# The loops of three edge layers written out, and part of the weighing of gathered rows moved from VectorE to ScalarE

## The reference

```python
h = relu(layernorm(x)); x = x + L0(h)   # edge MLP, 20 kinds of products per edge, segment sum
h = relu(layernorm(x)); x = x + L1(h)   # GAT, 4 heads of 64
h = relu(layernorm(x)); x = x + L2(h)   # sum of edge_weight * (h @ w_nbr)[src], + h @ w_own + bias
h = relu(layernorm(x)); x = x + L3(h)   # graph transformer block, 8 heads of 32, two batch norms, MLP

# L1 (L3 alike, with another score and 8 heads)
e = leaky_relu(es[src] + ed[dst]); m = segment_max(e, dst)
ex = exp(e - m[dst]); alpha = ex / segment_sum(ex, dst)[dst]
out = segment_sum(alpha[:, :, None] * z[src], dst)
```

## Time and profile before

| | |
|---|---|
| median of 3 runs | 8612.5 us (8587.99 to 8642.88) |
| profiled execution, its time | 8678.63 us |
| its span | 8676.9 us |
| PE, PE weight loads, DVE busy | 68%, 50%, 60% of the span |
| ACT, POOL busy | 23%, 44% |
| mean granted TensorE clock | 0.788 |

### The profile page before, as it was taken

One profiled execution on the slowest core, in us unless ns is written; L12 is line 12 of the kernel. 1 busy time (PEld: TensorE's weight loads), 2 busy tenths in 40 slices (PEclk: granted clock), 3 DMA queues, 4 the chain that ended last, 5 costly groups with the idle time before them and its releaser, 6 DMA issues. The chain is left out here.

```text
span 8676.9 us, 128745 instructions
## 1 busy us (share of the span) xinstructions
PE 5902.0 (68%) x29234; PEld 4310.6 (50%) x29235; DVE 5168.6 (60%) x12724; ACT 1984.6 (23%) x6402; POOL 3831.7 (44%) x4450
## 2 busy tenths in 40 slices
PE   2289999999999645555556555555845555555864
PEld 1178888888888533333334333333323333333553
DVE  4757777777776445665664444444326666777445
ACT  1045555555554311111112000000111111111232
POOL 1013333333333066666660666666026656675000
PEclk7589999999999867777778666666967767777587
DMA  2121111111111333333321233333033323232200
GB/s 76 43 81 53 51 51 53 51 51 53 51 52 50 114 96 89 85 87 83 86 73 58 86 90 90 90 90 89 28 92 85 82 74 82 79 89 67 62 6 31
DMA packets 319334, 606.56 MB, mean 70 GB/s; under 512 B 92201, under 2 KB 195565, under 8 KB 318719
## 3 DMA queue, kind: packets, MB, share of 16 engines
q0 software_dynamic: 171200, 474.81, 19.8%
q1 hardware_dynamic: 140746, 123.45, 4.7%
q10 hardware_dynamic: 7200, 6.56, 0.2%
HBM read 548.80 MB, written 62.98 MB: 71 GB/s over the span
## 5 line engine op out<-in xcount | busy, mean ns | idle before, releaser
L288 POOL DMA_INDIRECT G<-table,ib x1760 | 1917.2, 1089 | 470.5 <-issue 470.5
L186 POOL DMA_INDIRECT G<-table,ib x1760 | 1684.1, 957 | 470.2 <-issue 470.2
L560 PE MATMUL pM<-G,one 128*128 128x260 f32 (+1 forms) x3520 | 1282.1, 485 | 603.5 <-issue 212.1
L215 DVE TENSOR_TENSOR acc<-acc,pM 128x512 f32 (+1 forms) x1760 | 967.1, 549 | 600.2 <-DMA xr<-x 292.0
L560 PEld LDWEIGHTS pM<-G,one 128*128 128x128 f32 x3520 | 651.8, 221 | 1092.6 <-DVE acc L425 547.8
L425 DVE TENSOR_TENSOR acc<-acc,pM 128x260 f32 (+1 forms) x1760 | 758.0, 431 | 670.6 <-PE pM L560 391.7
L638 PE MATMUL pM<-G,one 128*128 128x256 f32 x1760 | 702.3, 550 | 592.3 <-DVE one L628 405.7
L1278 ACT ACTIVATE oh<-one,a4S 128x128 f32<-128x128 f32 x2640 | 861.6, 389 | 1.1 <-issue 0.9
L638 PEld LDWEIGHTS pM<-G,one 128*128 128x128 f32 x1760 | 427.2, 267 | 867.4 <-DVE one L628 462.1
L1357 PE MATMUL pM<-prod,oh 128*128 128x64 f32 x3520 | 681.9, 275 | 0.0
L479 ACT ACTIVATE oneT<-pT 128x512 bf16<-128x512 f32 x440 | 261.8, 597 | 1771.3 <-PE pT L544 893.9
(11 more groups left out here) (309 smaller groups left out, 8619.1 us busy)
## 6 DMA issues: line engine op xcount, KB each, us to landing
G<-table,ib POOLq DMA_INDIRECT x3520
far<-step_rec SPq DMA_DIRECT2D x224, 64.0 KB
table<-row SPq DMA_DIRECT2D x100, 128.0 KB
table<-row SPq DMA_DIRECT2D x50, 132.0 KB
table<-row SPq DMA_DIRECT2D x50, 130.0 KB
base<-aux SPq DMA_DIRECT2D x50, 128.0 KB
bs<-base SPq DMA_DIRECT2D x50, 128.0 KB
x<-xo ACTq DMA_DIRECT2D x50, 128.0 KB
```

The source lines that it names most:

```text
L186: pool.indirect_dma_start(G[j][:, :], None, rows, bass.IndirectOffsetOnAxis(ap=ib[:, j:j + 1], axis=0)).then_inc(s_g[j], 16)
L215: nc.vector.tensor_tensor(at, at, pM[j % R][:, :], ALU.add).then_inc(s_acc, 1)
L288: pool.indirect_dma_start(G[:, par * C + j, 0:ROW], None, tab, bass.IndirectOffsetOnAxis(ap=ib[:, par * C + j:par * C + j + 1], axis=0)).t ...
L560: nc.tensor.matmul(pM[j % R][:, :], one[:, par * C + j, :], G[:, par * C + j, :], start=True, stop=True).then_inc(s_m, 1)
```

## The change

Three edits. `steps` passes K // u turns as written out in layer 2 (u = 16), so that its loop is gone; layer 0 (u = U = 8) keeps its loop. `over_chunks` calls every chunk in turn, with no loop, in layers 1 and 3. And the last QA quads of a full chunk (3 in layer 1, 2 in layer 3) are weighed by ACT: for each step and head one activation of 64 (layer 1) or 32 (layer 3) columns whose scale is the head's column of `G`. DVE weighs the first QV = 8 - QA. The last chunk has four quads, which DVE weighs.

```diff
-            with eng.Fori(peel, count // unroll) as i:
-                turn(i, False)
+            if peel < count // unroll:
+                with eng.Fori(peel, count // unroll) as i:
+                    turn(i, False)
...
-            pipelined(eng, K, u, 1, *parts)
+            pipelined(eng, K, u, 1 if u == U else K // u, *parts)
...
+            QA = 3 if H == 4 else 2
+            QV = C4 - QA
...
-                    for a_ in range(3):
-                        do(a_, a_ % 2, C, C if a_ else 0)
-                    with eng.Fori(1, (NC - 2) // 2) as i:
-                        for r_ in (1, 2):
-                            do(2 * i + r_, r_ % 2, C, C)
-                    for a_ in range(NC - 1, NC + 1):
-                        do(a_, a_ % 2, TAIL if a_ < NC else 0, C if a_ < NC else TAIL)
+                    for a_ in range(NC + 1):
+                        do(a_, a_ % 2, C if a_ < NC - 1 else TAIL if a_ < NC else 0, 0 if a_ == 0 else TAIL if a_ == NC else C)
...
                                 for q in range(nq):
-                                    weigh(b_, 1 - par, q)
+                                    if q < QV:
+                                        weigh(b_, 1 - par, q)
...
+                        def weigh(b_, par, q):
+                            act.wait_ge(s_al, b_ + 1)
+                            F = D // H
+                            for j in range(par * C + 4 * q, par * C + 4 * q + 4):
+                                for h in range(H):
+                                    ins = nc.scalar.activation(G[:, j, h * F:(h + 1) * F], G[:, j, h * F:(h + 1) * F], ACT.Copy,
+                                                               scale=G[:, j, D + h:D + h + 1])
+                            ins.then_inc(s_wa, 1)
...
-                            for q in range(3, mq):
-                                turned(a_, par, q)
+                            for q in range(3, C4):
+                                if q < mq:
+                                    turned(a_, par, q)
+                                if q - 3 < QA and 4 * (QV + q - 3) < n_b:
+                                    weigh(b_, 1 - par, QV + q - 3)
...
-                            if j % 4 == 0:
-                                pe.wait_ge(s_msg, C4 * b_ + j // 4 + 1)
+                            if j % 4 == 0 and j // 4 < QV:
+                                pe.wait_ge(s_msg, QV * b_ + j // 4 + 1)
+                            elif j % 4 == 0:
+                                pe.wait_ge(s_wa, QA * b_ + j // 4 - QV + 1)
```

More of the change, by code:

```diff
@@ L253, in edge_attention @@
                     se.sem(n) for n in ("s_R", "s_f", "s_bt", "s_al", "s_msg", "s_m", "s_acc", "s_rs", "s_v", "s_z", "s_rows", "s_i", "s_part"))
-                s_ed = se.sem("s_ed")
+                s_ed, s_wa = se.sem("s_ed"), se.sem("s_wa")
                 s_g = [se.sem(f"s_g{z}") for z in range(2 * C4)]
```

## The result

The changed kernel takes 8999.26 us (median of 4, 8986.29 to 9023.51), the kernel before, run beside it, 8623.76 us: ratio 1.0444, 95% interval 1.0401 to 1.0487. It is slower by 4.4%, where the prediction said 8130 us. Its profiled execution took 9023.51 us.

A forecast was written before the change was run, and what follows sets the result against it. It took POOL to bound layers 1 and 2 after the change, ACT's queue to brake layer 3. 165 + 193 + 150 = 508 us off 8678.6 (profiled) or 8612.5 (median) gives 8171 or 8105; it took 8130, range 8000 to 8330.

The forecast's parts named there:

- the supply of instructions after a jump: Layers 1 to 3: DVE's slow instructions, 0.70 us each, begin behind the loop's branch and last some 17 us.
- The jump goes, and with it the slow stretch: Layer 2 written out: no slow stretch, POOL bounds at 1126 us for 1291, -165 us.
- its like in layer 1 and 3: Layers 1 and 3 without jumps, ScalarE's weighs included: -193 us in layer 1, -150 us in layer 3.
- The sign of ScalarE's part: Layer 1: moved weighs pay by leaving POOL alone; three would have cost it 2.3 us more a chunk.
- POOL's interference: Layer 1: DVE's weighs and marks delay POOL, 0.75 us a weigh, 0.25 a mark; POOL bounds at 46.5 us a chunk.
- ACT as its brake: Layer 3: queued activations make PE wait; PE and DVE lose 5.5 us a chunk, win 1.4, giving 51.2 us.
- (4): Layers 1 and 3: written-out code from memory brings a slow stretch with each new page, 9050 us; chance 0.06.
- (2): Slow stretches don't hang on the jump and would stay in layer 2, 165 us more, 8295 us; chance 0.08.
- (1): Layer 3: ACT is no brake, activations cost 0.15 us or less, POOL bounds, 8026 us; chance 0.14.
- (3): Layers 1 to 3: straight code loses too, though less, 220 us more, 8350 us; chance 0.17.

The follow-up runs named there:

- only2: Changed kernel with layers 1 and 3 back in loops and all weighs on DVE, only layer 2 written out: 1.0004 of before, without stretches.
- only_act: Kernel before, all loops kept, with only ScalarE's weighs added in layers 1 and 3: 1.0145 of before, on a chip without stretches.
- all_dve_2: Changed kernel without ScalarE's part: loops written out, DVE weighs all eight quads; on a chip with stretches, 0.9804 of before.
- split: Written-out loops; idle ScalarE activations, later last weighs left out. Layer 3, with stretches: 51.1 us a chunk with all weighs, 61.6 with two missing.
- after_3: The changed kernel unaltered, run again on a chip without stretches: 8124.63 us, 1.0034 of before.
- all_dve: Changed kernel without ScalarE's part: loops written out, DVE weighs all eight quads; on a chip without stretches, 0.9994 of before.
- thin: Written-out loops, all weighs on DVE, layer 2 gathers 64 of 256 columns: 0.9997, then 0.9975, without stretches. As a sum in probe: 651 us.
- probe: Changed kernel with layer 2's sum replaced by eight 448-step sums, each with one thing changed; with stretches, the sums took 645 to 661 us.
- plain: The sum of probe that runs as in the changed kernel, 448 steps, on a chip with stretches: 650 us.

## Why the prediction was wrong

**The step that failed** is "I take the slow stretches for the supply of instructions after a jump", and with it "The jump goes, and with it the slow stretch" (layer 2, -165) and its like in layer 1 and 3. The reading under it, that the slow instructions "begin right behind the branch", was wrong too. In layer 2 of before, 224 of the 254 sequencer instructions over 0.5 us (the node loads left out) come 8 us or more behind DVE's last branch. One turn, the branch and the next sequencer instruction, then adds:

```profile
L133 DVEq COMPARE_BRANCH  x1: 56/56/56, 5156.1 to 5156.1; - x1
L133 DVEq FUSED_REGOPS  x1: 74/74/74, 5156.4 to 5156.4; - x1
```

```profile
5164.47 0.42 DVE L215 TENSOR_TENSOR acc<-acc,pM 128x256 f32 x1
...
5171.11 0.42 DVE L215 TENSOR_TENSOR acc<-acc,pM 128x256 f32 x1 [3.54 <-issue]
```

Between 5158 and 5164.47 the adds are 0.63 to 0.86 us apart, and the first slow one stands 8.5 us behind the branch, 9 into POOL's run of gathers. A loop's turn there is as long as a cycle of POOL's: run of gathers, stretch, pause of POOL (in 45 of 53 it begins 19 to 20 us behind DVE's branch), catch-up. The two were locked, and I took the one for the cause of the other. In layers 1 and 3 the order is the other way round. The long chunk of the earlier trace rows (3709.87 to 3772.15) lost most of its time ahead of its jump, the largest piece 17 us before it, where an add comes 8.7 us behind the one before:

```profile
3750.68 0.42 DVE L425 TENSOR_TENSOR acc<-acc,pM 128x260 f32 x1 [7.15 <-remote]
```

In layer 3 chunk 2 took 72.1 us before DVE had jumped at all. What a jump itself costs is the time from the branch to the next sequencer instruction, 3.1 us in layer 1 and 0.3 in layer 2, and it is the same on chip 9, without stretches (only2, only_act):

```profile
L264 DVEq COMPARE_BRANCH  x1: 68/68/68, 3767.8 to 3767.8; - x1
L264 DVEq FUSED_REGOPS  x1: 126/126/126, 3770.9 to 3770.9; - x1
```

The written-out layer 2 has no jump and a cycle of 28.8 us of its own. Gain in layer 2: 24 us (1291 to 1267) for 165; with loops written out and nothing else, in the profiled executions, layer 1 gained 27 x 2.2 = 59 us for 193, layer 3 27 x 6.0 = 162 (all_dve_2 against before). (The two traces may be of two chips, both with stretches.) What the runs put in its place: on some chips the engines beside POOL get late some 10 us into a run of gathers and are fast again about three us after POOL stops, in loops and in straight code alike, so that layer 2 takes some 1.44 us a step for the 1.27 I forecast.

The trace of before had shown it without any jump. Ahead of layer 1's first chunk POOL issues 64 gathers in a row (3055 to 3137 us), DVE has nothing to do from 3075 on, the code is written out, and ACT's `turned` comes ever later behind PE's product. Three rows of ACT:

```profile
3099.09 0.60 ACT L479 ACTIVATE oneT<-pT 128x512 bf16<-128x512 f32 x1 [11.99 <-DMA a_pad<-zf]
3120.09 0.60 ACT L479 ACTIVATE oneT<-pT 128x512 bf16<-128x512 f32 x1 [20.40 <-issue]
3141.79 0.60 ACT L479 ACTIVATE oneT<-pT 128x512 bf16<-128x512 f32 x1 [21.10 <-DMA a_pad<-zf]
```

In only2, on chip 9, the same rows stand 2.4 us apart. So the lateness is not DVE's alone. From the first gather to the first scores before takes 90 us there and only2 44, and in layer 3 it is 96 and 44. All eight traces with stretches have it (67 to 92 us ahead of layer 1), and none of the twelve others (44 us). These some 100 us of before were in none of my terms, and no edit of the change touches them.

**The sign of ScalarE's part.** I wrote that the moved weighs "pay here by leaving it alone", POOL that is. On a chip with stretches taking the weighs away is what costs: 8 to 9 us a chunk in layer 1, 7 to 12 in layer 3 (table), and split shows it in layer 3 with ACT idle. Without stretches the step holds: 2.5 us a chunk less in layer 1.

**The sum, where there are no stretches.** after_3 took 8124.63 us for 8130. Layer 2: 1123 us for 1126. Layer 1: 1199 us for 1415 - 193 = 1222; DVE waits for gathers as forecast, and POOL's interference was put 1.9 us a chunk too high (44.6 for 46.5). Layer 3: 1408 us for 1377, 52.5 us a full chunk for 51.2, with ACT as its brake: in the chunk from 6312.6 us PE waits 4.8 us for `oneT`, where I had 5.5. A row of ACT there:

```profile
6282.57 6.88 ACT L485 ACTIVATE G<-G 128x32 f32<-128x32 f32 x32
```

The quad took 6.88 us for my 7.0. (The Trainium skill, "ScalarE: Activation LUTs", What ACT_TABLE_LOAD costs, gave 6.8; less the last activation's 0.31 the row's 31 intervals are 0.212 us each for its 0.213, so the trace agrees.) But on those chips before takes 8078 to 8083 us: the 508 us that I meant to win were mostly stretches, and there they are gone without any edit. That 8130 was met there is luck. The misses in layers 1 and 3 (23 us too high, 31 too low) nearly cancel, and the change is worth nothing on such a chip.

**What I overlooked.** I explained the profiled execution's lying 36 us over the highest run by stretches, and so knew that they vary between executions. I did not ask whether they vary between chips.

**Rivals.** (4) gave 9050 us, and 8999 came: right in size, wrong in mechanism, since written-out code alone is 2.0% faster. I gave it 0.06 for the reason that chunks 0 to 2 ran well in straight code. That held for layer 1 alone (layer 3's chunk 2 took 72.1 us), and they ran well with all weighs on DVE, which the change takes away. (2), that the stretches don't hang on the jump, is what is true; its 8295 us put the stretches back in layer 2 only, and did not see that they stay, and grow, in layers 1 and 3. (Of the page cited with it, the Trainium skill, "Runtime: NRT & Kernel Launch", Instruction fetch mechanics: that a branch within two pages does not stall agrees with the 0.3 us at each jump of layer 2; the 3.1 us in layer 1, whose turn has 428 instructions of DVE in the trace, no run decides. I had written that row and page differ. It was my reading of the row that did.) (1) and (3) were not met. Of what I had said the profile would show, the activations came 0.24 and 0.21 us apart, about as forecast (0.25 and 0.22). That DVE had no sequencer instruction of 0.7 us came true too and meant nothing, because the lateness then lies between the rows.

**Open.** What makes the engines late, whether POOL's pace alone decides it, and why writing out the loops gains 2.0% on such a chip, most of it in layer 3. It is not bytes, register instructions, the amount of fetched code or buffers, and a pause of 0.42 us per four gathers is not enough. One mark tells the two kinds of chip apart in all twenty traces, before and after among them: on those with stretches the profile has no landing time for the gathers, since part of the events that mark it are missing. (The trace of the changed kernel holds 34169 events of DMA landings and 55584 of semaphores, that of after_3, the same code, 73290 and 97941. They are missing in layer 0 too, which has no stretch.) The row of DMA issues on the page of the changed kernel, then on that of after_3 (the last number is the median us from issue to landing):

```profile
G<-table,ib POOLq DMA_INDIRECT x3520
```

```profile
G<-table,ib POOLq DMA_INDIRECT x3520, 2.8
```

So what carries events or semaphores may be what is full on those chips; that is a guess. Every execution here, timed ones too, has a recorded span and clock; whether the stretches would be there without any recording, no run here can tell.

## What to carry to other kernels

Before you cost a stall as removable, find out what ends it, not only what stands at its start: here the slow stretches ended some three us after POOL stopped, and a loop that had locked to this cycle looked like their cause. Look also for the stall where its supposed cause is absent: the straight code ahead of the first chunk held it, and with it the answer. Work that delays another engine can be what keeps the rest in step, so before moving it, try the kernel with that work simply left out. And see before and after on more than one chip: this change is 4.3% slower on one and the same within 0.7% on another, while written-out loops with all weighs on DVE are 0.980 on the first and 0.999 on the other, the best of those that compute everything and were timed on both.

## What the hardware showed that I had not expected

- The same kernel before took 8081, 8078 and 8083 us on two chips and 8624 to 8638, 8736 and 8770 on others, at like granted clocks (0.787 to 0.795 on chip 9, 0.785 to 0.794 on chip 12). The difference lies in layers 1 to 3 alone; layer 0, where in before 880 gathers start between 563.07 and 2796.90 us, 2.54 us apart, had no stretch.
- Leaving two of eight 1.2-us weighs out lengthened a chunk from 51.1 to 61.6 us on a chip with stretches.
- A hand-over from PE to ACT took up to 19 us (3122.45 to 3141.79 in before) while GpSimd issued 64 gathers in a row and VectorE did nothing; the same one takes under 0.1 us in only2.
- A gather of 128 rows costs POOL 1.27 us whether a row has 256 columns or 64 (layer 2 in 1121 and 1120 us, all_dve and thin), at 103 GB/s or 26. With stretches the two are alike as well. The windows of probe, plain and thin:

```profile
4946.00:5600.00 654.00, 356.46 (x896) 195.98 (x896) 298.71 (x896) 22.58 (x110) 450.20 (x559) 0.67 0.31 90
...
6274.00:6928.00 654.00, 362.20 (x896) 204.45 (x896) 297.12 (x891) 22.58 (x110) 447.98 (x559) 0.65 0.12 23
```

- A stall of DVE's sequencer need not show in any duration: in the changed kernel the row ahead of the add reads 57 ns throughout layer 2, and 0.7 us and more lay between such rows.
